# A whitening kernel: weights folded into the last matrix product, the norm given three more slots, and stores of 128 partitions, two per image, on GpSimd and at the end on SyncE

## The chip, the cores and the metric

The kernel runs on one core of one Trainium2 chip. The metric is the device time in microseconds. An execution taken with the hardware profiler gives the rows that are read below.

## What is computed

32 images of 256 channels and 48 x 48 pixels are whitened and then mixed by a 32 x 32 weight. Channel c belongs to group member c mod 32, so each image is a matrix of 32 rows and 8 x 2304 columns.

```python
x1 = x.reshape(N, C // G, G, H, W).transpose(0, 2, 1, 3, 4).reshape(N, G, -1)   # G = 32
xc = x1 - x1.mean(-1, keepdims=True)
cov = xc @ xc.transpose(0, 2, 1) / M + EPS * jnp.eye(G)
# isqrt_newton_schulz(cov, 10):
Y, Z = cov / normA, I                    # normA: the Frobenius norm
for _ in range(10):
    T = 0.5 * (3.0 * I - Z @ Y)
    Y, Z = Y @ T, T @ Z
decorr = Z / jnp.sqrt(normA)
y = weight1 @ decorr @ xc + bias1
```

## The kernel before

All is float32. An image stands in SBUF as 128 partitions of 2 x 2304 numbers (channels 0 to 127 and 128 to 255), in one of ten slots (`xs`, the trace's `image`), and the output overwrites it there. Every engine has its instructions written out by hand in one order, with semaphores between them; there is no scheduler. Images go in pairs (16 pairs). The loop of every engine runs over the pairs c, and in each over six rounds j of four slots s (24 slots). Three pairs are in work at a time:

- pair c is centred, transposed and its covariance is summed: ScalarE takes a shift off each quarter of an image (`centre`, L220), VectorE transposes it in twelve pieces (`transpose`, L315), and TensorE multiplies each transposed tile with itself (`covariance`, L432, six pieces an image, two pieces a round);
- pair c - 1 goes through the chain of small matrices, one step a slot: `chain` on TensorE (L454 to L478) and on VectorE (L324 to L389). `STEP_AT` gives each step's slot: the norm at slot 1, the first product (`NEXT_0`, L460) at slot 3, then one step a slot up to `SPREAD` at slot 23. The norm takes a product on TensorE (L457), a root on ScalarE (`root`, L236, behind two centrings of round 0), and six operations on VectorE (L349 to L357), of which the fifth, L354, writes `t_mat`, for which L460 waits. The ten Newton steps alternate products `z y` (L462) and `factor (y z)` (L464); the last one makes z alone (L466); `FOLD` multiplies z with the weight (L468); `SPREAD` puts the result on all four blocks of 32 partitions with four products and makes the offset with two (L474, L476). VectorE then writes `apply_w` (L377) and `y_bias` (L379);
- pair c - 2 is put out: `output` on TensorE (L493, four products of 384 columns for each of twelve strips) and on ScalarE (L230, which adds the bias and writes the strip into the image's slot).

Of the four output products, the one from partition half `row` to half `half` reads and writes the image half `row ^ half`. So for the first 128 channels a slot holds the output in order, and for the last 128 with its two halves of 64 partitions exchanged. GpSimd stores an image when its six strips are there (`store`, L181 to L188) by three DMAs: one of 128 partitions and two of 64. The last image is stored in three pieces of two strips. SyncE issues the loads, four quarters an image (L171). From image 10 on it waits at L170 for the stores of the image that had the slot. VectorE's `covariance_out` and `GATHER` (L339 to L345) stand at the end of a pair and are touched only by one more operation.

## Time and profile before

| what | us |
|---|---|
| median of 3 runs | 467.77 (463.84 to 476.04) |
| the profiled execution, its own time | 462.93 |
| its span, first to last instruction | 461.0 |
| TensorE busy in it | 379.3 (82%) |
| ScalarE busy | 332.9 (72%) |
| VectorE busy | 329.4 (71%) |

The engines are PE (TensorE's products), PEld (its weight loads), DVE (VectorE), ACT (ScalarE), POOL (GpSimd) and SP (SyncE); L12 is line 12 of the kernel printed above. An arrow `a<-b` in a row is an instruction that writes a and reads b. A float32 product stands in the rows as two matmuls. Busy time overlaps between engines. Idle time of an engine counts only where somebody waits for it, so the lists of waits and the timeline are read beside it. The granted clock (PEclk) is 1.00 at 2.4 GHz and 0.50 at 1.2 GHz.

### The profile page before, as it was taken

The numbers are of one execution on the slowest core, as the hardware profiler recorded it, in microseconds if no ns is written. First come the engines' busy times: TensorE is split into PE (matmuls) and PEld (weight loads), VectorE is DVE, ScalarE is ACT, GpSimd is POOL, SyncE is SP. The second block draws the span as 40 slices with busy tenths as digits, with TensorE's granted clock in tenths as the row PEclk, the third lists the DMA queues.
The fourth block names the chain that finished last, engine by engine and source line by source line (L and its number), as shares of the span: only waits on it lengthen the run. The fifth ranks groups of instructions, "written<-read, shape, count | busy, mean of one in ns | idle before, by whom it ended". The sixth has DMA issues, their size and how long they took to land.

```text
span 461.0 us, 17013 instructions
## 1 busy us (share of the span) xinstructions
PE 379.3 (82%) x7392; PEld 271.3 (59%) x7392; DVE 329.4 (71%) x1033; ACT 332.9 (72%) x450; POOL 56.8 (12%) x108
## 2 busy tenths in 40 slices
PE   0868899898989899898989897989999897977700
PEld 0856766666657667675756665666767575633100
DVE  5767887797869777988868787779888786643000
ACT  5772478797969868787878787787878796455800
POOL 0000001111111111020111111111102011112500
PEclk9976999999999989999989999899999999999965
DMA  7999939999999999999999999999999666677990
GB/s 271 416 409 410 412 141 284 338 346 351 381 358 404 357 394 344 398 390 390 385 383 362 381 394 382 367 327 388 384 391 388 218 208 208 200 213 225 312 268 18
DMA packets 28747, 152.11 MB, mean 330 GB/s; under 512 B 3968, under 2 KB 3968, under 8 KB 20736
## 3 DMA queue, kind: packets, MB, share of 16 engines
q0 software_dynamic: 9952, 75.50, 46.6%
q1 hardware_dynamic: 18432, 75.51, 43.2%
q8 instruction: 58, 0.95, 0.8%
q14 instruction: 17, 0.14, 0.1%
q10 hardware_dynamic: 288, 0.01, 0.0%
HBM read 75.51 MB, written 75.50 MB: 328 GB/s over the span
## 4 chain that ended last, share of the span: by engine, by line
PE 67%; DVE 11%; ACT 8%; issue 5%; DMA 2%; POOL 1%; SPq 0%; DVEq 0%; POOLq 0%; ACTq 0%
PE cov_ps L432 29%; PE y_ps L493 25%; PE chain_ps L464 6%; ACT image L220 6%; DVE transposed L315 5%; PE chain_ps L462 2%; DMA image<-x 2%; PE cov_ps L444 1%; PE chain_ps L474 1%; POOL y L188 1%; DVE yz L353 1%; DVE t_mat L354 1%; DVE col L350 1%; ACT image L230 1%; PE chain_ps L466 1%
## 5 line engine op out<-in xcount | busy, mean ns | idle before, releaser
L315 DVE STREAM_TRANSPOSE transposed<-image 128x384 f32<-128x384 f32 x384 | 215.7, 572 | 13.5 <-ACT image L220 2.8
L230 ACT ACTIVATE image<-y_ps,y_bias 128x768 f32<-128x768 f32 x192 | 164.8, 894 | 68.4 <-PE y_ps L493 67.7
L432 PE MATMUL cov_ps<-transposed 128*64 128x65 f32 x4608 | 178.7, 231 | 5.4 <-issue 5.4
L493 PE MATMUL y_ps<-image,apply_w 64*64 64x384 f32 x1536 | 171.8, 513 | 4.4 <-issue 2.3
L432 PEld LDWEIGHTS cov_ps<-transposed 128*64 128x64 f32 x4608 | 160.9, 142 | 14.5 <-issue 6.3
L220 ACT ACTIVATE image<-image,shift 128x1152 f32<-128x1152 f32 x128 | 156.1, 1248 | 1.8 <-DMA image<-x 0.8
L493 PEld LDWEIGHTS y_ps<-image,apply_w 64*64 64x64 f32 x1536 | 58.9, 135 | 15.1 <-ACT image L230 7.6
L186 POOL DMA_DIRECT2D y<-image x34 | 19.4, 572 | 381.1 <-ACT image L230 381.1
L462 PEld LDWEIGHTS chain_ps<-yz 128*64 128x64 f32 (+1 forms) x288 | 32.8, 138 | 35.4 <-DVE yz L367 27.3
L367 DVE SCALAR_TENSOR_TENSOR yz<-yz,chain_ps 64x96 f32<-64x96 f32 x144 | 33.8, 234 | 22.9 <-PE chain_ps L464 16.9
L464 PE MATMUL chain_ps<-yz,t_mat 64*64 64x96 f32 x256 | 47.0, 265 | 3.4 <-DVE t_mat L362 3.4
L464 PEld LDWEIGHTS chain_ps<-yz,t_mat 64*64 64x64 f32 x256 | 27.3, 135 | 35.8 <-DVE t_mat L362 28.8
L462 PE MATMUL chain_ps<-yz 128*64 128x32 f32 (+1 forms) x288 | 37.9, 213 | 6.9 <-DVE yz L359 3.4
L188 POOL DMA_DIRECT2D y<-image x68 | 36.7, 545 | 0.2 <-issue 0.2
L362 DVE SCALAR_TENSOR_TENSOR t_mat<-chain_ps,parity 64x64 f32<-64x64 f32 x144 | 27.3, 190 | 10.0 <-PE chain_ps L462 8.0
L212 ACT COPY shift<-shift_ps 128x1 f32<-128x1 f32 x32 | 5.1, 158 | 27.1 <-PE shift_ps L420 27.1
L349 DVE RECIPROCAL col<-col 64x1 f32<-64x1 f32 x16 | 2.5, 155 | 28.1 <-ACT col L236 28.1
L460 PE MATMUL chain_ps<-yz,t_mat 64*64 64x32 f32 x32 | 4.9, 234 | 20.9 <-DVE t_mat L354 20.7
L460 PEld LDWEIGHTS chain_ps<-yz,t_mat 64*64 64x64 f32 x32 | 3.1, 135 | 31.2 <-DVE t_mat L354 31.2
L420 PE MATMUL shift_ps<-shift_sum,shift_mat 128*64 128x1 f32 x128 | 9.3, 196 | 12.3 <-ACT junk L206 12.3
L420 PEld LDWEIGHTS shift_ps<-shift_sum,shift_mat 128*64 128x64 f32 x128 | 7.4, 141 | 12.4 <-ACT junk L206 6.5
L206 ACT ACTIVATE junk<-image 128x288 bf16<-128x288 f32 x32 | 13.8, 433 | 0.0
(59 smaller groups left out, 167.1 us busy)
## 6 DMA issues: line engine op xcount, KB each, us to landing
image<-x SPq DMA_DIRECT2D x128, 576.0 KB, 11.2
y<-image POOLq DMA_DIRECT2D x31, 1152.0 KB, 8.6
y<-image POOLq DMA_DIRECT2D x62, 576.0 KB, 11.0
y<-image POOLq DMA_DIRECT2D x3, 384.0 KB, 12.2
y<-image POOLq DMA_DIRECT2D x6, 192.0 KB, 11.6
b_col<-bias ACTq DMA_DIRECT2D x4, 0.1 KB, 6.3
w_nat<-weight ACTq DMA_DIRECT2D x2, 4.0 KB, 4.3
```

Of the source, the lines that this page charges most:

```text
L186: pool.dma_start(out_v[n, :, 0, cols], slot[:, 0, cols]).then_inc(stored[n % SLOTS][0], 16)
L188: pool.dma_start(out_v[n, channels, 1, cols], slot[rows, 1, cols]).then_inc(stored[n % SLOTS][1], 16)
L220: nc.scalar.activation(part, part, ACT.Identity, bias=shift[:, n % 2:n % 2 + 1]).then_inc(centred, 1)
L230: nc.scalar.activation(xs[n % SLOTS][:, :, STRIP * q:STRIP * (q + 1)], y_ps[:, f % 2, :, 0:STRIP], ACT.Identity, bias=y_bias[:, c % 2, i:i ...
L315: nc.vector.transpose(xt[q][:, TILES // 2 * part:TILES // 2 * (part + 1), 0:CH], xs[n % SLOTS][:, h, at:at + TWELFTH]).then_inc(transposed, 1)
L362: link(nc.vector.scalar_tensor_tensor(out=factor, in0=product.unsqueeze(1).to_broadcast([Q, PAIR, G]), scalar=-0.5, in1=own, op0=ALU.mult, ...
L367: link(nc.vector.scalar_tensor_tensor(out=yz[0:Q, first:YZ], in0=yz[0:Q, first:YZ], scalar=1.5, in1=following[:, first:YZ], op0=ALU.mult, ...
L420: ins = nc.tensor.matmul(shift_ps[HALF * half:HALF * (half + 1), 0:1], shift_mat[:].rearrange("p m g -> p (m g)"), shift_sum[:, n % 2:n % ...
L432: ins = nc.tensor.matmul(cov_ps[rows, n % 2, 0:GRAM], xt[q][:, t, 0:CH], xt[q][:, t, 0:GRAM], start=q == 0 and t < 2, stop=q == IMAGE_PIEC ...
L462: ins = nc.tensor.matmul(chain_ps[0:Q, C_PRODUCT:C_PRODUCT + G], z, y, start=True, stop=True)
L464: ins = nc.tensor.matmul(chain_ps[0:Q, C_NEXT:C_NEXT + YZ], factor, both, start=True, stop=True)
L493: ins = nc.tensor.matmul(y_ps[out_rows, f % 2, h, 0:STRIP], apply_w[rows, c % 2, i].rearrange("p k g -> p (k g)"), xs[n % SLOTS][rows, h, ...
```

## The change

- The steps are fewer by two. The weight (`w_t`) now stands beside y and z in one tile (`wyz`), and the last step (`LAST`) multiplies z with `w_t` and y in one product of 64 columns. VectorE makes from it `t_wide` (the last Newton factor) and `folded` (the weighted z, scaled), and `SPREAD` is one product of the two for each half of the partitions.
- The offset is no longer part of `SPREAD`. `gather` makes the means of both images (one more product), VectorE copies them into `means` (one more operation of `GATHER`), and a new step `offset` multiplies them with `apply_w` (four products of one column on TensorE, one operation on VectorE) in slot 0 of the next pair. ScalarE's first output and TensorE's next norm product wait for it (`offset_dve`).
- The norm's product goes from slot 1 to slot 2, VectorE's part to slot 4, `NEXT_0` to slot 5: three slots stand between the norm's product and `NEXT_0`. ScalarE's `root` stands behind the first evacuation of its round, no longer ahead of it, and `half_root` one round later.
- The output product from partition half `row` to half `half` now reads image half `half` and writes half `row`. So a slot holds channels r * 64 to r * 64 + 63 (first 64 partitions) and 128 + r * 64 on (last 64). One image is two DMAs (r = 0, 1), each of all 128 partitions in SBUF, and of 2 runs of 64 channels in HBM. GpSimd issues those of images 0 to 29, SyncE those of 30 (whole) and 31 (in three pieces), behind its loads.

```diff
-STEP_AT = {1: NORM, 3: NEXT_0} | {t + 1: t for t in range(NEXT_0 + 1, SPREAD + 1)}
+OFFSET_AT, NORM_AT, NORM_OUT_AT, NEXT_0_AT = 0, 2, 4, 5
...
-    out_v = out.rearrange("n (h p) a b -> n p h (a b)", h=HALVES)
+    out_v = out.rearrange("n (o r p) a b -> n r o p (a b)", o=HALVES, r=2)
...
+        def store(engine, n, pieces, signals):
+
+            engine.wait_ge(y_read, IMAGE_PIECES * n + pieces.stop)
+            cols = slice(STRIP * pieces.start, STRIP * pieces.stop)
+            for r in range(2):
+                engine.dma_start(out_v[n, r, :, :, cols], xs[n % SLOTS][:, r, cols]).then_inc(signals[r], 16)
...
+            for n in range(IMAGES):
+                load(n)
+            for n in range(IMAGES - PAIR, IMAGES):
+                for q in range(0, IMAGE_PIECES, IMAGE_PIECES // PARTS[n]):
+                    store(sp, n, slice(q, q + IMAGE_PIECES // PARTS[n]), [stored_last] * 2)
+            sp.wait_ge(stored_last, 16 * 2 * sum(PARTS.values()))
...
-                pool.dma_start(out_v[n, :, 0, cols], slot[:, 0, cols]).then_inc(stored[n % SLOTS][0], 16)
-                for rows, channels in ((slice(0, HALF), slice(HALF, P)), (slice(HALF, P), slice(0, HALF))):
-                    pool.dma_start(out_v[n, channels, 1, cols], slot[rows, 1, cols]).then_inc(stored[n % SLOTS][1], 16)
...
+            for n in range(IMAGES - PAIR):
+                store(pool, n, slice(0, IMAGE_PIECES), stored[n % SLOTS])
...
+                    if exists(c - 2):
+                        output(c - 2, 2 * j)
                     if j == 0 and exists(c - 1):
                         root(c - 1)
-                    if exists(c - 2):
-                        output(c - 2, 2 * j)
...
+                elif t == LAST:
+
+                    weighted, product = product, chain_ps[0:Q, C_PRODUCT + G:C_PRODUCT + 2 * G]
+                    link(nc.vector.scalar_tensor_tensor(
+                        out=t_wide[:], in0=product.unsqueeze(1).to_broadcast([Q, 2, G]), scalar=-0.5, in1=eye15_wide[:],
+                        op0=ALU.mult, op1=ALU.add))
+                    link(nc.vector.scalar_tensor_tensor(
+                        out=folded[:], in0=weighted.unsqueeze(1).to_broadcast([Q, PAIR, G]), scalar=RSQ, in1=own,
+                        op0=ALU.mult, op1=ALU.mult))
...
+            def offset(c):
+
+                pe.wait_ge(chain_dve, OPS_TOTAL * (c + 1))
+                for half in range(2):
+                    for i in range(PAIR):
+                        ins = nc.tensor.matmul(chain_ps[HALF * half:HALF * (half + 1), C_OFFSET + i:C_OFFSET + i + 1],
+                                               apply_w[:, c % 2, i].rearrange("p k g -> p (k g)"),
+                                               means[:, c % 2, i:i + 1], start=True, stop=True)
+                ins.then_inc(offset_pe, 1)
...
-                        h = row ^ half
-                        ins = nc.tensor.matmul(y_ps[out_rows, f % 2, h, 0:STRIP], apply_w[rows, c % 2, i].rearrange("p k g -> p (k g)"),
-                                               xs[n % SLOTS][rows, h, STRIP * q:STRIP * (q + 1)], start=True, stop=True)
+                        ins = nc.tensor.matmul(y_ps[out_rows, f % 2, row, 0:STRIP],
+                                               apply_w[rows, c % 2, i].rearrange("p k g -> p (k g)"),
+                                               xs[n % SLOTS][rows, half, STRIP * q:STRIP * (q + 1)],
+                                               start=True, stop=True)
```

The order of TensorE's instructions at the begin of a pair with all three stages, before:

```order
L432 MATMUL cov_ps<-transposed 64x65 x12
L420 MATMUL shift_ps<-shift_sum,shift_mat 64x1 x2
L432 MATMUL cov_ps<-transposed 64x65 x12
L457 MATMUL chain_ps<-col,parity 64x1
L493 MATMUL y_ps<-image,apply_w 64x384 x8
L460 MATMUL chain_ps<-yz,t_mat 64x32
L432 MATMUL cov_ps<-transposed 64x65 x12
L462 MATMUL chain_ps<-yz 64x32
L432 MATMUL cov_ps<-transposed 64x65 x12
L464 MATMUL chain_ps<-yz,t_mat 64x96
```

The same place now (L456 is the covariance, L524 the output, L485 the norm's product, L488 `NEXT_0`, L508 the offset):

```order
L456 MATMUL cov_ps<-transposed 64x65 x12
L508 MATMUL chain_ps<-means,apply_w 64x1 x4
L444 MATMUL shift_ps<-shift_sum,shift_mat 64x1 x2
L456 MATMUL cov_ps<-transposed 64x65 x12
L524 MATMUL y_ps<-image,apply_w 64x384 x4
L485 MATMUL chain_ps<-col,parity 64x1
L524 MATMUL y_ps<-image,apply_w 64x384 x4
L456 MATMUL cov_ps<-transposed 64x65 x24
L488 MATMUL chain_ps<-wyz,t_mat 64x32
L524 MATMUL y_ps<-image,apply_w 64x384 x4
L490 MATMUL chain_ps<-wyz 64x32
L524 MATMUL y_ps<-image,apply_w 64x384 x4
```

Two covariance pieces now stand between the output products and `NEXT_0`.

GpSimd's queue before, from its first store on; the three DMAs of an image (L186 once, L188 twice) recur to the end:

```order
L178 AFFINE_SELECT eye<-eye 128x128
L186 DMA y<-image 128x2304
L188 DMA y<-image 64x2304 x2
L186 DMA y<-image 128x2304
L188 DMA y<-image 64x2304 x2
```

GpSimd's queue now:

```order
L202 MEMSET eye 128x128
L204 ISA
L204 AFFINE_SELECT eye<-eye 128x128
L179 DMA y<-image 2x64x2304 x60
L88 UNCONDITIONAL_BRANCH
```

And SyncE's queue now, where before there were the loads alone:

```order
L181 UNCONDITIONAL_BRANCH
L190 DMA image<-x 128x1152 x128
L179 DMA y<-image 2x64x2304 x2
L179 DMA y<-image 2x64x768 x6
L88 UNCONDITIONAL_BRANCH
```

The sizes are those of the side that is written, slowest dimension first: a store's began with 128 or 64 and now begins with 2.

## Rows read from the trace of the kernel before

**Rows 1.** The page, busy time and share of the span by engine.

```profile
PE 379.3 (82%) x7392; PEld 271.3 (59%) x7392; DVE 329.4 (71%) x1033; ACT 332.9 (72%) x450; POOL 56.8 (12%) x108
```

**Rows 2.** Windows: length, busy PE, PEld, DVE, ACT, POOL, PEclk, DMA share, GB/s.

```profile
282.06:307.94 25.88, 23.98 (x469) 17.23 (x466) 20.54 (x64) 20.61 (x28) 3.39 (x7) 0.93 0.99 366
307.94:332.23 24.29, 22.40 (x470) 16.28 (x468) 20.43 (x64) 20.50 (x29) 3.30 (x7) 1.00 1.00 372
332.23:356.50 24.27, 22.54 (x468) 16.27 (x466) 20.43 (x64) 20.54 (x28) 3.27 (x7) 1.00 1.01 388
```

**Rows 3.** Who waited for whom: us in total, times, longest.

```profile
DVE col L349 <- ACT col L236: 28.1, 16, 3.0
PE chain_ps L460 <- DVE t_mat L354: 20.7, 14, 2.5
ACT image L220 <- DMA image<-x: 0.8, 2, 0.4
```

**Rows 4.** Timeline of two pairs: start, us, engine, line, [idle before].

```profile
287.28 1.38 PE L432 MATMUL cov_ps<-transposed 128*64 128x65 f32 x23
...
307.94 2.40 ACT L220 ACTIVATE image<-image,shift 128x1152 f32<-128x1152 f32 x2
308.53 1.48 PE L493 MATMUL y_ps<-image,apply_w 64*64 64x384 f32 x13
310.25 0.15 ACT L236 ACTIVATE col<-chain_ps 64x1 f32<-64x1 f32 x1
...
311.39 0.22 DVE L354 SCALAR_TENSOR_TENSOR t_mat<-yz,parity 64x64 f32<-64x64 f32 x1
311.66 0.30 PE L460 MATMUL chain_ps<-yz,t_mat 64*64 64x32 f32 x2 [1.66 <-DVE t_mat L354]
311.89 0.92 PE L432 MATMUL cov_ps<-transposed 128*64 128x65 f32 x24
313.05 0.24 PE L462 MATMUL chain_ps<-yz 128*64 128x32 f32 x1 [0.24 <-DVE yz L359]
```

**Rows 5.** The window with loads only, columns as in rows 2.

```profile
10.00:50.00 40.00, 29.16 (x595) 26.17 (x596) 29.36 (x82) 25.06 (x35) 0.00 (x0) 0.83 1.02 412
```

**Rows 6.** SyncE's wait for stores; timeline of image 8's store and its slot's next use.

```profile
SPq L171 <- DMA y<-image: 231.4, 44, 26.1
...
170.76 0.57 POOL L186 DMA_DIRECT2D y<-image  x1 [13.82 <-ACT image L230]
...
217.80 0.43 ACT L206 ACTIVATE junk<-image 128x288 bf16<-128x288 f32 x1
```

**Rows 7.** DMA: packets, queues (packets, MB, share of 16 engines), issues (median us to landing).

```profile
DMA packets 28747, 152.11 MB, mean 330 GB/s; under 512 B 3968, under 2 KB 3968, under 8 KB 20736
q0 software_dynamic: 9952, 75.50, 46.6%
q1 hardware_dynamic: 18432, 75.51, 43.2%
image<-x SPq DMA_DIRECT2D x128, 576.0 KB, 11.2
y<-image POOLq DMA_DIRECT2D x62, 576.0 KB, 11.0
```

**Rows 8.** Timeline of the end: image 30's first issue, the last evacuation and the last issue.

```profile
424.95 0.57 POOL L186 DMA_DIRECT2D y<-image  x1 [7.75 <-ACT image L230]
...
435.26 1.69 ACT L230 ACTIVATE image<-y_ps,y_bias 128x768 f32<-128x768 f32 x2 [0.20 <-PE y_ps L493]
...
437.81 1.07 POOL L188 DMA_DIRECT2D y<-image  x2
```

**Rows 9.** The last window in which packets move, columns as in rows 2.

```profile
451.00:452.00 1.00, 0.00 (x0) 0.00 (x0) 0.00 (x0) 0.00 (x0) 0.00 (x0) 0.50 0.06 25
```

**Rows 10.** Groups by line, with busy us and mean ns of one.

```profile
L230 ACT ACTIVATE image<-y_ps,y_bias 128x768 f32<-128x768 f32 x192 | 164.8, 894 | 68.4 <-PE y_ps L493 67.7
L466 PE MATMUL chain_ps<-yz,t_mat 64*64 64x64 f32 x32 | 5.2, 242 | 0.4 <-DVE t_mat L362 0.4
```

More of the change, by code:

```diff
@@ L113, in whiten @@
         d_col = sb("d_col", [Q, 1])
-        d_mask = sb("d_mask", [Q, PAIR])
+        means = sb("means", [P, 2, PAIR])
         outer = sb("outer", [Q, G])
@@ L150, in whiten @@
         chain_act = sem("chain_act")
+        offset_pe = sem("offset_pe")
+        offset_dve = sem("offset_dve")
         y_done = sem("y_done")
@@ L161, in quarter_of, with load @@
             return xs[n % SLOTS][:, h, QUARTER * o:QUARTER * (o + 1)]
+        def store(engine, n, pieces, signals):
[3 more added lines that the diff above has]
+                engine.dma_start(out_v[n, r, :, :, cols], xs[n % SLOTS][:, r, cols]).then_inc(signals[r], 16)
         @block.sync
         def _(sp):
-            for n in range(IMAGES):
+            def load(n):
                 for p in range(QUARTERS):
@@ L291, in _ @@
             dve.wait_ge(shift_mat_ready, 1)
-            for zeros in (yz, t_mat, parity):
+            for zeros in (wyz, t_mat, parity, means):
                 then(nc.vector.memset(zeros[:], 0.0))
@@ L302, in _ @@
             then(nc.vector.tensor_scalar(eye15[:], eye[0:Q, 0:Q], 1.5, None, ALU.mult))
-            for i in range(PAIR):
-                then(nc.vector.tensor_copy(pick[:, i], eye[0:Q, G * i:G * (i + 1)].unsqueeze(1).to_broadcast([Q, 2, G])))
+            then(nc.vector.tensor_scalar(eye15_wide[:], eye_col[0:Q, :].unsqueeze(1).to_broadcast([Q, 2, G]), 1.5, None,
+                                         ALU.mult))
+            then(nc.vector.tensor_scalar(mean_mat[:], eye_col[:].unsqueeze(1).to_broadcast([P, 2, G]), 1.0 / SAMPLES,
+                                         None, ALU.mult))
             def transpose(n, k):
@@ L398, in _ @@
                     j = s // SLOTS_A_ROUND
-                    if s in STEP_AT and exists(c - 1):
-                        chain(c - 1, STEP_AT[s])
+                    if s == OFFSET_AT and exists(c - 2):
+                        offset(c - 2)
+                    if s in DVE_AT and exists(c - 1):
+                        chain(c - 1, DVE_AT[s])
                     if s == 9 and exists(c):
@@ L469, in chain @@
                 else:
                     for half in range(2):
-                        out_rows = slice(HALF * half, HALF * (half + 1))
-                        for i in range(PAIR):
-                            at = C_SPREAD + G * i
-                            nc.tensor.matmul(chain_ps[out_rows, at:at + G], pick[:, i].rearrange("p b g -> p (b g)"),
-                                             folded[:, 0, :], start=True, stop=True)
-                        ins = nc.tensor.matmul(chain_ps[out_rows, C_OFFSET:C_OFFSET + PAIR],
-                                               folded[:].rearrange("p b g -> p (b g)"), d_mask[:],
-                                               start=True, stop=True)
@@ L479, in chain, with offset @@
-                ins.then_inc(chain_pe, 1)
+                        ins = nc.tensor.matmul(chain_ps[HALF * half:HALF * (half + 1), C_SPREAD:C_SPREAD + PAIR * G],
+                                               t_wide[:].rearrange("p k g -> p (k g)"),
+                                               folded[:].rearrange("p i g -> p (i g)"), start=True, stop=True)
+                ins.then_inc(chain_pe, 1)
+            def offset(c):
+                pe.wait_ge(chain_dve, OPS_TOTAL * (c + 1))
[5 more added lines that the diff above has]
+                ins.then_inc(offset_pe, 1)
@@ L506, in _ @@
                         covariance(PAIR * c + 2 * j // IMAGE_PIECES, 2 * j % IMAGE_PIECES)
-                    if s in STEP_AT and exists(c - 1):
-                        chain(c - 1, STEP_AT[s], slice(0, P) if exists(c) else slice(0, Q))
+                    if s == OFFSET_AT and exists(c - 2):
+                        offset(c - 2)
+                    if s in PE_AT and exists(c - 1):
+                        chain(c - 1, PE_AT[s], slice(0, P) if exists(c) else slice(0, Q))
                     ahead = PAIR * c + 1 + j // 3
@@ L514, in _ @@
                     for m in range(1, SLOTS_A_ROUND):
-                        if s + m in STEP_AT and exists(c - 1):
-                            chain(c - 1, STEP_AT[s + m], slice(0, Q))
+                        if s + m in PE_AT and exists(c - 1):
+                            chain(c - 1, PE_AT[s + m], slice(0, Q))
                         if m < 3 and exists(c - 2):
```

96 lines of the change are left out of this document (45 added, 51 removed).

## The prediction

> **What bounds the kernel now.** I read the page first: the span is 461.0 us, TensorE is busy for 82% of it, and VectorE and ScalarE for some 72% each [rows 1]. No engine is full on average, so the stages have to be told apart. The windows of single pairs show how: an undisturbed pair takes 24.29 us, of which TensorE is busy for 22.40, VectorE for 20.43 and ScalarE for 20.50 [rows 2]. TensorE is the nearest to full, and the list of waits says what it lacks: it waits for `t_mat` of L354 before L460 (20.7 us on 14 occasions), while VectorE waits before L349 for ScalarE's root (28.1 us on 16) [rows 3]. The timeline of one pair shows it as a chain: ScalarE centres two quarters from 307.94, the root at L236 stands behind them and starts at 310.25, VectorE's norm follows and starts `t_mat` at 311.39, and TensorE, whose output products began at 308.53 and took 1.48 us, starts L460 only at 311.66, 1.66 us idle; then 0.24 us more before L462 [rows 4].
>
> Some pairs take 25.88 us at a granted clock of 0.93 in place of 1.00 [rows 2]: a part of them ran at the lower level, 1.2 GHz. The trace has three such pairs in the twelve between 81 and 382 us, and each costs 25.88 - 24.29 = 1.6 us. In the one that begins at 282.06, 23 covariance products take 1.38 us from 287.28 on, where 24 take 0.92 in the pair above [rows 4].
>
> DMA is the other thing to read. Beside the pairs it moves 366 to 388 GB/s with a busy share of 0.99 to 1.01 [rows 2], hardly below the 412 GB/s of the stretch in which there are loads only [rows 5]. Yet ScalarE waits for a load only 0.8 us in all [rows 3], because the ten slots give a lead. Image 8's store is issued at 170.76; its slot, filled with image 18, is first read at 217.80, 47.0 us later [rows 6]. In these 47.0 us lie the issue (1.7 us), the landing of the store (median 11.0 us for a half) and of the load (11.2 us) [rows 7]: 24 us, so 23 us are spare. At the end ScalarE's last evacuation runs from 435.26 to 436.95, GpSimd issues until 438.9 [rows 8], the last packets move in the window 451 to 452 [rows 9], and the span goes on for 9 us more.
>
> **The change part by part.**
>
> *Norm with three free slots.* L460's product is moved behind two more covariance pieces (0.92 us each on the timeline, some 1.7 together, as their edges overlap) [rows 4]. The root goes behind one evacuation (0.894 us [rows 10]). Root: 310.25 + 0.86 = 311.1. From its start to `t_mat` ready took 311.61 - 310.25 = 1.36 us, so `t_mat` is ready at 312.5. TensorE would be there at 310.0 + 1.7 = 311.7. The wait shrinks from 1.66 + 0.24 to about 0.75 us, a gain of 1.15. What is late next is still this root, now because of ScalarE's queue. Bounds: 0 gained (if the root slips by as much as TensorE's place) and 1.9.
>
> *Weights folded into the last product.* Per pair one L462 and the L466 (242 ns [rows 10]) go, and L468 becomes a product of 64 columns; six products of the spreading become two, but four offset products and one for the means are added. I take 0.2 us for the L466, whose end overlaps with what follows, and set the other pieces equal (bounds 0 and 0.6). VectorE loses four small operations of the chain and gets three. It isn't the bound: 20.43 busy [rows 2] and the pauses between its 64 instructions (24.29 - 20.43 less about 2.2 of waits = 1.7) make 22.1.
>
> So a pair would take 24.29 - 1.15 - 0.2 = 22.9 us. Over 14 pairs that is 20 us; half of the slow-clock cost goes with the shorter idle (2.4); the first and the last pair, bound by the chain of matrices, lose a step each (1.5). Sum 24 us, if transfers keep up. An added wait is `offset_dve` ahead of L457's successor: behind it stands TensorE's whole queue, but VectorE's bias is one short operation ahead of four transposes, and a covariance piece of 0.92 us and an output stand between the offset products and that wait, so I price it at nothing (bounds 0 and 0.4 us a pair).
>
> *The stores.* Three DMAs an image become two on GpSimd. Its issue (1.7 us an image) is off the path until the end; there, with SyncE issuing, 1.1 to 2 us go, or 3 with a quicker landing. The decisive point is another. The HBM side of every new store starts with a dimension of 2 (`2x64x2304`), where every DMA of the kernel before starts with 128, 64 or 32 rows. The packets show how those are cut: SyncE's queue has 18432 packets for 128 loads, which is 128 x (128 rows + 16), and the 3968 packets under 512 B are 16 for each of the 128 loads and the 102 stores, and 6 x (32 + 16) for ScalarE's six small loads [rows 7]. So each DMA is handed out in 16 equal shares of whole rows. A division by the outermost dimension finds only 2 equal shares in the new stores. No row of before shows such a DMA, so both ways stay open: 16 shares (nothing changes) and 2. I take 2 as the likelier.
>
> The Trainium skill, "DMA: Bandwidth & Descriptors", section "Why a DMA increments its semaphore by 16 and not by 1", says that the number of engines is the largest up to 16 that divides the slowest non-1 dimension of both sides, and "Rules for kernel authors" warns of an outermost dimension under 16; by that rule these stores get 2 engines, and SyncE's always the lowest-numbered ones. The same table advises one 128-partition transfer over two on halves, which by itself would speak for the change. The trace agrees with the rule as far as it goes (16 closing packets for outer sizes 128, 64 and 32) and has no case of 2.
>
> What 2 shares cost. One engine moves 412/16 = 25.8 GB/s in the loads-only stretch [rows 5]; all of the stores' packet time gives 75.50 MB / (0.466 x 461.0 us x 16) = 22.0 GB/s [rows 7]. I take 24.
>
> At the end: images 30 and 31 are 2 x 2359 KB = 4719 KB; over 2 engines at 24 GB/s that is 98 us (91 at 25.8, 107 at 22.0), against 26 us now from the issue at 424.95 to 451.5 [rows 8, 9]. This takes the same two engines for all eight of SyncE's stores, since they come from one queue and have one form; on changing pairs each would take only its own 590/24 = 25 us, the lower bound of this term.
>
> In the middle: one share is 590 KB. Alone on its engine it takes 590/25.8 = 23 us; if the loads first take all they ask (2359/16 = 147 KB an image each 11.45 us, or 12.9 GB/s) it takes 590/12.9 = 46 us. I take 34, the middle. Loads on a shared engine land later too: 14 us for 11.2. Then issue, store and load need 1.2 + 34 + 14 = 49 us where, at 22.9 us a pair, 47.0 x 22.9/24.3 = 44.3 are there. Loads become late, and the half pair stretches to 49/47.0 x 12.15 = 12.7 us, 25.3 a pair, near the 25.1 that the twelve pairs between 81 and 382 us take on average now (with their slow stretches): the gain in the middle is given back. Bounds: all 20 us kept (store in 23 us), or 28 us a pair, 35 us lost.
>
> Sum: image 30's store starts at 424.95 - 5 (what the first and last pairs keep, with a little of the middle) = 420; 98 us of stores, 5 us for GpSimd's shares still on those two engines, 9.5 us after the last packet: span 532.5, and 1.9 around it (462.93 - 461.0): 534.4, said as **535 us**. The profiled execution (462.93) is 4.8 us under the median of the three runs, 467.77; I add nothing for that. About 2% is what a measurement of this kernel can tell from no change.
>
> **The rivals.**
>
> *A. All stores use 16 shares; faster.* 24 us from the pairs and 3 at the end: 462.9 - 27 = 436. For it: whole-row cutting by partitions would be as natural, and SBUF's side does have 128 rows. It needs 9437 KB in 22.9 us, 412 GB/s, above the 388 of any pair; the 23 us of spare lead pay for a shortfall of 1.1 us a pair over 11 pairs (12 us), else up to 12 us come back: 436 to 448.
>
> *B. Only SyncE's stores get 2 shares.* The page calls GpSimd's queue a software and SyncE's a hardware one [rows 7], so they may cut differently. Image 30's store then starts at 424.95 - 24 = 401: 401 + 98 + 9.5 + 1.9 = 510.
>
> *C. 16 shares, and the norm's wait only moves.* The root behind the evacuation slips as far as L460 does; 5 to 8 us remain of the 24: 455 to 460, within 2%.
>
> **How the numbers follow.** Forecast (2 shares on both queues) 0.58, B 0.08, A 0.28, C 0.06. Slower 0.66, faster 0.28, same 0.06. The forecast's own range is 500 to 575: from 395 + 91 + 11.4 to 450 + 107 + 15 with the bounds of the middle. As A holds more than 2 in 10, and changing pairs of engines would end near 450, the range that is to hold 8 in 10 reaches down into it: 430 to 570.
>
> **What would show it.** Right: the page's issue table has SyncE's `y<-image` landing after 50 to 95 us and GpSimd's after 25 to 45, not 11; after the last evacuation some 80 us in which no engine works and DMA's share is near 2/16 = 0.13; a wait of ScalarE's centring for `image<-x` in the pairs; SyncE waits longer for stores than 231.4 us [rows 6]. The norm step: VectorE's wait for the root before its first reciprocal falls from 28.1 us to about 20, TensorE's for `t_mat` from 20.7 to about 10; in a pair without late loads 22.9 us. Wrong: landings near 10 us and a DMA share near 1 to the end mean A; GpSimd's near 10 and SyncE's long mean B; pairs of 24 us with short landings mean C.

## The result, and the profile after

The changed kernel takes 627.25 us (median of 4 runs, 622.4 to 639.11), the kernel before beside it 467.82 (463.84 to 476.04): 1.341 times as long, 95% interval 1.327 to 1.356. The direction and the cut into two shares were forecast; 535 us and the range up to 570 were not enough. The profiled execution took 622.4 us, its span 620.5. Runs of one kernel fall into a faster and a slower group, 2 to 6% apart: ratios and intervals are of the faster runs, and the profiles of experiments 3, 4, 6, 8 and 14 are of one of the slower.

The page of the changed kernel, first the busy time (it answers to [rows 1]), then the 40 slices (15.5 us each) of clock, DMA share and GB/s:

```profile
PE 401.1 (65%) x7360; PEld 277.0 (45%) x7360; DVE 323.1 (52%) x1018; ACT 334.8 (54%) x450; POOL 47.9 (8%) x66
...
PEclk9978998968979888989879879797789997555555
DMA  8999259898989989999899899898776686311110
GB/s 311 411 411 392 72 146 267 258 305 313 300 269 304 305 263 281 336 296 276 318 331 324 288 286 309 249 270 278 231 232 210 189 220 189 107 74 50 51 52 40
```

Two losses can be seen at once. The slices 7 to 30 move 231 to 336 GB/s, where [rows 2] had 366 to 388; and in the last four some 50 GB/s are left, after TensorE's last work, at a clock of 0.5. DMA view of the changed kernel, as in [rows 7]:

```profile
DMA packets 82234, 152.31 MB, mean 245 GB/s; under 512 B 57072, under 2 KB 57072, under 8 KB 74224
## 3 DMA queue, kind: packets, MB, share of 16 engines
q0 software_dynamic: 62400, 71.00, 40.4%
q1 hardware_dynamic: 19472, 80.22, 34.1%
q8 instruction: 58, 0.95, 0.6%
...
image<-x SPq DMA_DIRECT2D x128, 576.0 KB, 18.7
y<-image POOLq DMA_DIRECT2D x60, 1152.0 KB, 42.0
```

SyncE's queue has 19472 packets: 18432 for the loads as before, and 1040 for its 8 stores, 130 each: 128 rows and 2 closing packets, not 16. So the new stores are cut in two. GpSimd's stores land after 42.0 us (11.0 in [rows 7]), the loads after 18.7 (11.2).

Windows of the changed kernel (columns as in [rows 2]); the first two are a pair's length each in the middle, the others lie behind the last evacuation, which ends at 516:

```profile
281.32:313.57 32.25, 24.57 (x453) 16.81 (x450) 20.01 (x62) 20.60 (x29) 3.14 (x4) 0.90 0.93 301
313.57:340.69 27.12, 24.71 (x477) 17.32 (x479) 20.32 (x62) 20.83 (x29) 3.14 (x4) 0.93 1.00 324
525.00:550.00 25.00, 0.00 (x0) 0.00 (x0) 0.00 (x0) 0.00 (x0) 0.00 (x0) 0.50 0.35 110
550.00:575.00 25.00, 0.00 (x0) 0.00 (x0) 0.00 (x0) 0.00 (x0) 0.00 (x0) 0.50 0.13 52
```

A DMA share of 0.13 is 2 engines of 16, and 52 GB/s over them is 26 GB/s each. Waits of the changed kernel (us in total, times, longest); L364, L488, L369 and L232 are the L349, L460, L354 and L220 of [rows 3], and L218 sums the pixels for the shift:

```profile
ACT image L232 <- DMA image<-x: 68.8, 31, 6.3
DVE col L364 <- ACT col L248: 63.9, 16, 14.1
ACT junk L218 <- DMA image<-x: 37.2, 11, 11.0
PE chain_ps L488 <- DVE t_mat L369: 15.5, 10, 5.2
```

ScalarE now waits 106 us for loads, where it waited 0.8. VectorE's wait for the root grew to 63.9 us because ScalarE reaches the root late, when a load in front of it is late: with the same order of instructions and without late loads (experiment 1) it is 18.4 us. So its length says nothing of the norm step here.

How late becomes a time is read from the chain that ended last, changed kernel (start, us, what):

```profile
281.32 37.95 DMA y<-image
...
319.28 2.08 SPq L190
...
321.41 1.88 SPq L190
...
323.33 1.85 SPq L190
...
325.22 30.92 DMA image<-x
```

Image 14's store is issued at 281.32 and lands 37.95 us later; only then SyncE issues the loads into its slot, some 2 us each, and the last quarter needed lands at 356.14, 74.8 us after the store was issued. The same piece from 196.45 on is a store of 44.95, SyncE's issues and a load of 29.14, to 277.64: 81.2 us, after which the chain comes to the store at 281.32, 3.7 us later. Between the stores of image 9 and image 14 five images pass in 84.9 us, 17 each. The last turn, from the store at 359.83 on, is longer and carries seven images: the store takes 44.18 us, then SyncE needs 51.9 us to get to the last of 12 loads (29.8 of them are waits whose end the profile can't name), and that load lands at 473.49. All of the middle goes at about one pace: GpSimd's store of image 4 is at 115.94 and that of image 25 at 462.78, 16.5 us an image, 33 us a pair.

The loss can be split in two by the kernel of experiment 1, which has 64-row halves, the same compute side and a span of 445.2 us. GpSimd's last issue starts at 504.31 in the changed kernel and at 419.40 in that one, 85 us apart; from there to the end of the span the changed kernel needs 116.2 us and the other 25.8, 90 us apart.

### The profile page after: what moved, and what is told of

It is laid out like the page before. It is cut to its first block, busy times and chain, and to the rows that moved or that the text cites. A ratio compares the mean times of both kernels' runs of the same rounds, so it can differ in the third digit from the quotient of the medians.

```text
span 620.5 us, 16900 instructions
## 1 busy us (share of the span) xinstructions
PE 401.1 (65%) x7360; PEld 277.0 (45%) x7360; DVE 323.1 (52%) x1018; ACT 334.8 (54%) x450; POOL 47.9 (8%) x66
## 2 busy tenths in 40 slices
DMA packets 82234, 152.31 MB, mean 245 GB/s; under 512 B 57072, under 2 KB 57072, under 8 KB 74224
## 3 DMA queue, kind: packets, MB, share of 16 engines
q0 software_dynamic: 62400, 71.00, 40.4%
q1 hardware_dynamic: 19472, 80.22, 34.1%
## 4 chain that ended last, share of the span: by engine, by line
DMA 46%; PE 16%; SPq 7%; another core or an unknown queue 5%; ACT 4%; DVE 3%; issue 2%; ACTq 0%; DVEq 0%
DMA y<-image 28%; DMA image<-x 18%; SPq L190 7%; PE cov_ps L456 7%; PE y_ps L524 6%; ACT image L242 2%; PE chain_ps L492 2%; ACT image L232 1%; DVE transposed L329 1%; ACT junk L218 0%; PE chain_ps L490 0%; DVE wyz L381 0%; DVE t_mat L377 0%; PE cov_ps L468 0%
## 5 line engine op out<-in xcount | busy, mean ns | idle before, releaser
L232 ACT ACTIVATE image<-image,shift 128x1152 f32<-128x1152 f32 x128 | 157.0, 1250 | 69.8 <-DMA image<-x 68.8
L524 PE MATMUL y_ps<-image,apply_w 64*64 64x384 f32 x1536 | 187.1, 553 | 10.4 <-ACT image L242 9.1
L456 PE MATMUL cov_ps<-transposed 128*64 128x65 f32 x4608 | 183.2, 236 | 10.6 <-issue 10.5
L456 PEld LDWEIGHTS cov_ps<-transposed 128*64 128x64 f32 x4608 | 166.6, 147 | 30.4 <-issue 20.0
L179 POOL DMA_DIRECT2D y<-image x60 | 47.2, 790 | 457.2 <-ACT image L242 457.1
L524 PEld LDWEIGHTS y_ps<-image,apply_w 64*64 64x64 f32 x1536 | 57.2, 142 | 20.6 <-ACT image L242 16.6
L381 DVE SCALAR_TENSOR_TENSOR wyz<-wyz,chain_ps 64x96 f32<-64x96 f32 x128 | 30.3, 237 | 53.3 <-PE chain_ps L492 53.2
L492 PE MATMUL chain_ps<-wyz,t_mat 64*64 64x96 f32 x256 | 47.5, 267 | 4.3 <-DVE t_mat L377 3.4
L492 PEld LDWEIGHTS chain_ps<-wyz,t_mat 64*64 64x64 f32 x256 | 28.5, 139 | 38.0 <-DVE t_mat L377 26.9
L490 PEld LDWEIGHTS chain_ps<-wyz 64*64 64x64 f32 (+1 forms) x256 | 30.0, 142 | 32.9 <-DVE wyz L381 18.9
L377 DVE SCALAR_TENSOR_TENSOR t_mat<-chain_ps,parity 64x64 f32<-64x64 f32 x128 | 25.4, 199 | 21.3 <-PE chain_ps L490 18.6
L490 PE MATMUL chain_ps<-wyz 64*64 64x32 f32 (+1 forms) x256 | 34.2, 216 | 3.2 <-DVE wyz L381 2.7
L364 DVE RECIPROCAL col<-col 64x1 f32<-64x1 f32 x16 | 2.5, 155 | 63.9 <-ACT col L248 63.9
L218 ACT ACTIVATE junk<-image 128x288 bf16<-128x288 f32 x32 | 14.0, 436 | 37.3 <-DMA image<-x 37.2
L224 ACT COPY shift<-shift_ps 128x1 f32<-128x1 f32 x32 | 4.9, 154 | 26.8 <-PE shift_ps L444 26.8
L488 PE MATMUL chain_ps<-wyz,t_mat 64*64 64x32 f32 x32 | 5.3, 247 | 15.6 <-DVE t_mat L369 15.5
L488 PEld LDWEIGHTS chain_ps<-wyz,t_mat 64*64 64x64 f32 x32 | 3.4, 148 | 18.2 <-DVE t_mat L369 17.9
L485 PEld LDWEIGHTS chain_ps<-col,parity 64*64 64x64 f32 x32 | 5.1, 165 | 8.7 <-issue 7.4
## 6 DMA issues: line engine op xcount, KB each, us to landing
image<-x SPq DMA_DIRECT2D x128, 576.0 KB, 18.7
```

The source lines that it names most:

```text
L179: engine.dma_start(out_v[n, r, :, :, cols], xs[n % SLOTS][:, r, cols]).then_inc(signals[r], 16)
L232: nc.scalar.activation(part, part, ACT.Identity, bias=shift[:, n % 2:n % 2 + 1]).then_inc(centred, 1)
L377: link(nc.vector.scalar_tensor_tensor(out=factor, in0=product.unsqueeze(1).to_broadcast([Q, PAIR, G]), scalar=-0.5, in1=own, op0=ALU.mult, ...
L381: link(nc.vector.scalar_tensor_tensor(out=yz[0:Q], in0=yz[0:Q], scalar=1.5, in1=following, op0=ALU.mult, op1=ALU.add))
L456: ins = nc.tensor.matmul(cov_ps[rows, n % 2, 0:GRAM], xt[q][:, t, 0:CH], xt[q][:, t, 0:GRAM], start=q == 0 and t < 2, stop=q == IMAGE_PIEC ...
L490: ins = nc.tensor.matmul(chain_ps[0:Q, C_PRODUCT:C_PRODUCT + G], z, y, start=True, stop=True)
```

## The experiments

All are edits of the changed kernel unless said otherwise, and each ran beside the kernel before on its chip (medians 463.81 us beside experiments 1 to 4, 467.95 beside 5 to 8, 470.52 beside 9 to 12, 465.53 beside 13 and 14).

**1. Every new store in two of 64 rows.**

```diff
-                engine.dma_start(out_v[n, r, :, :, cols], xs[n % SLOTS][:, r, cols]).then_inc(signals[r], 16)
+                for o in range(HALVES):
+                    engine.dma_start(out_v[n, r, o, :, cols], xs[n % SLOTS][HALF * o:HALF * (o + 1), r, cols]).then_inc(
+                        signals[r], 16)
```

with the counts of the waits for `stored` doubled.

> The changed kernel, but each of its stores is cut into two DMAs of 64 channels, so that the HBM side starts with 64 and no longer with 2; queues, layout and all of the compute stay. Theory 'shares' (the stores with an outermost dimension of 2 ran on two engines, and that alone made the kernel slower): stores land in about 11 us on GpSimd, no idle stretch at the end, 436 to 448 us, 5% under the kernel before. Rival 'compute' (the new chain, norm and offset order lose time in the middle, where pairs take 33 us in the changed kernel): pairs stay near 33 us, over 500 us.

Measured: 447.2 us (446.22 to 454.01, 4 runs), 0.963 times the kernel before, interval 0.954 to 0.972. Same bytes, same order, same issuing engines: 180 us less than the changed kernel. DMA issues of this kernel:

```profile
image<-x SPq DMA_DIRECT2D x128, 576.0 KB, 14.0
y<-image POOLq DMA_DIRECT2D x120, 576.0 KB, 9.7
y<-image SPq DMA_DIRECT2D x4, 576.0 KB, 6.4
```

The whole loss is the form of the stores. The halves also made each DMA smaller; experiment 4 leaves the size alone.

**2 and 3. Halves for GpSimd's stores only, and for SyncE's only.** GpSimd stores the images up to 29, SyncE the rest, so the edit of experiment 1 goes under a condition, and the other engine keeps 2 x 64:

```diff
+                if n < IMAGES - PAIR:
```

and in the second kernel `n >= IMAGES - PAIR`.

> As rows64, but only GpSimd's stores (images 0 to 29) are cut into 64 channels; SyncE's for the last pair keep the outermost dimension of 2. 'Shares': the middle is that of rows64, the last evacuation comes near 410, and then two engines need 4719 KB / 52 GB/s = 91 us from image 30's issue on: 500 to 510 us. Rival 'SyncE's long end only follows from GpSimd's backlog on the same engines': then the end shrinks to some 20 us and the time is 440 to 455.

Measured: 530.65 us (529.51 to 531.79), 83 us over experiment 1. GpSimd's stores land after 9.2 us, the last evacuation ends at 437.9, and the page's last slices move 46 to 59 GB/s: the tail alone. The 500 to 510 us that I expected were too few, because the last evacuation was to end near 410.

> As the changed kernel, but SyncE's stores of the last pair are cut into 64 channels; GpSimd's keep the 2. 'Shares': the middle stays as in the changed kernel (last evacuation near 515), then 15 to 25 us until the last packet: 535 to 550 us. So the two parts of the loss are about 80 us each, and rows64_gpsimd and rows64_synce together account for it.

Measured: 554.46 and 584.67 us; I compare 554.46, 107 us over experiment 1. In the profiled run, that of 584.67, GpSimd's stores land after 44.0 us and ScalarE's centring waits 115.4 us for loads. The parts, 83 and 107, make 190 us where the whole loss is 180: both queues cut by the outermost dimension, and within the spread of these runs the two losses add.

**4 to 6. Other outermost dimensions with whole-tile stores.** One number differs, `o=HALVES` in `out_v` becomes 16, 4 or 8 (the output's rows then come in another order). The three texts stand in the order 16, 4, 8.

> The changed kernel with one number changed: the HBM side of a store is (16, 8, columns) and no longer (2, 64, columns), still 128 partitions and two DMAs an image. Rows land on other channels than they should, all of them once, so the output is permuted. 'Shares by the outermost dimension': 16 shares, landing near 11 us, within 1% of rows64. Rival 'a store whose HBM side is not one even run of rows is slow' (the pattern, not the first number): it stays near 620 us.

Measured: 448.95 us (440.52 to 456.09), ratio 0.954 (0.939 to 0.969). The 128-partition store is as good as two halves once its HBM side starts with 16.

> The HBM side of the stores is rearranged as 4 x 32 rows instead of 2 x 64; the rows of the output come out in another order, every byte count and every wait is as in the changed kernel. Theory (engines = shares of the outermost dimension, and the loss is made of late slots): 4 engines a store, so SyncE's tail is 4719 KB over 4 x 26 GB/s = 45 us instead of 91-100, from image 30's store at 405 to 425 on (the kernel with 64-row halves issues it at 425.8). In the middle a share is 295 KB; GpSimd's stores land in 18 to 25 us, loads in 12 to 14, so issue + store + load = 32 to 41 us, under the 47 that are spare: pairs stay near 24 us. Together 460 to 485 us, and the packets of SyncE's 8 stores are 8 x (128 + 4). Rival 1 (the small packets that a GpSimd store of few shares puts on the other engines cost time of their own, and there are 12/14 x 33/65 of them, 0.44 as many): 0.44 of the 78 us lost in the middle stay, 34 us more: 495 to 520. Rival 2 (only the number 2 is special): near the 447 of the halves kernel.

> As before with 8 x 16 rows on the HBM side (output rows in another order). Theory: 8 engines, a share of 147 KB, tail 4719 KB over 8 x 26 GB/s = 23 us, which is about what the two last images take with all 16 engines beside the last loads and evacuations; GpSimd's stores land in 11 to 14 us. 445 to 458 us. Rival 1 (small packets): 0.15 of 78 us stay, 12 us more: 457 to 470. SyncE's packets are 8 x (128 + 8).

Measured: 546.5 us with 4 shares (2 runs, ratio 1.170, 1.159 to 1.182), and 495.77 and 526.9 us with 8, of which the run of 526.9 was profiled. Both lie far over the forecast of the theory, and the loss is not where the rival put it: ScalarE's centring waits for loads only 0.9 and 0.5 us. What waits is TensorE, and for nothing that the profile shows. Chain by engine, kernel with 8 shares:

```profile
PE 65%; issue 14%; DVE 8%; ACT 5%; DMA 2%; SPq 0%; ACTq 0%; DVEq 0%
```

Here 14% is 74 us; the kernel before has 4.7% of 461, 22 us. With 4 shares the longest piece is this, in the middle of a group of output products (timeline of TensorE, then the DMA view of 340 to 342 us, the same kernel):

```profile
333.58 0.83 PE L524 MATMUL y_ps<-image,apply_w 64*64 64x384 f32 x3
344.08 0.90 PE L524 MATMUL y_ps<-image,apply_w 64*64 64x384 f32 x2 [9.67 <-issue]
```

```profile
q8 instruction: 1, 0.02, 3.0%
```

Nothing stands between two products of one group except the next instruction. The page has a queue q8 of kind "instruction" with 58 packets in every kernel that has a program on TensorE, and its 0.95 MB make 16 KB a packet; in the four kernels without one (experiments 9, 10, 13 and 14) this queue is not there. Looked up microsecond by microsecond, its packets mostly come 4 to 9 us apart; where a long stall is, one is late, and the stall ends 2 to 3 us behind it. With 4 shares the packets after 318 us are in the microseconds from 318, 325 and 341, and the stall ends at 344.08; the five other stalls of 5 to 8.7 us end at 127.6, 162.8, 184.8, 233.4 and 446.8, with packets from 125, 160, 182, 231 and 444 on. With 8 shares the longest, 7.21 us, ends at 308.7, and the packet is in 306 to 307. It holds without exception: each of TensorE's issue waits of more than 1 us, 15 with 4 shares and 18 with 8, ends 2.4 to 3.4 us after the begin of a packet's microsecond. So TensorE stops for its code. That the code is late because the stores' shares load the DMA engines is what experiment 12 tests. In profiled spans the kernel with 4 shares has its last evacuation end 62 us later than experiment 1 (493.5 for 431.4) and needs 38 us more from there to its end; with 8 shares these are 66 and 14. TensorE's issue waits are 46 us more in both profiles (64 for 18): they are most of what was lost ahead of the last evacuation in these runs.

**7. Nine slots in the changed kernel** (`SLOTS = 9`).

> The changed kernel with 9 image slots in place of 10. From a slot's first read to its store's issue the kernel before needs 5 pairs less 47.0 us, i.e. 74.5 us or 3.07 pairs of 24.29 us; what is left of the slot's cycle is issue + store + load, L. With 10 slots the cycle is 5 pairs, so a pair takes L / 1.93; the changed kernel has L = 1.7 + 42.0 + 18.7 = 62.4 us, which gives 32.3 us a pair (33 are measured in the middle). Theory 1 (the time is set by lateness, landing times fixed by the shares): with 9 slots the cycle is 4.5 pairs, a pair takes 62.4 / 1.43 = 43.6 us, 10.6 us more over some 12 pairs: about 750 us, with landings still near 42 and 18.7. Theory 2 (the two engines a store and the small packets set a throughput, and the landing times are only what queues up): pairs stay at 33 us, 615 to 640 us, and landings fall by 16.5 us together, to some 30 and 14. Between the two: a pair of 36 to 39 us, 670 to 700, if landings fall by part.

Measured: 687.81 and 706.47 us, median 697.1; stores land after 41.5 us and loads after 18.2, as with ten slots; 18.6 us an image (37.2 a pair). Chain of this kernel:

```profile
229.63 46.73 DMA y<-image
276.75 2.12 SPq L190
278.91 2.64 SPq L190
281.59 22.67 DMA image<-x
307.94 39.60 DMA y<-image
347.56 14.03 DMA image<-x
363.34 43.05 DMA y<-image
```

A throughput that alone sets the pace is out: the landings did not shorten, and the time rose by 70 us. From store to store the chain takes 78.3 us from 229.63 to 307.94, about what it took with ten slots (84.9), but only four images pass in it, not five. My scaling of the wait by pairs (43.6 us a pair) was too steep, which comes back below; the later turns of 55 to 58 us carry three images.

**8. The root ahead of the evacuation again**, on top of experiment 1.

```diff
-                    if exists(c - 2):
-                        output(c - 2, 2 * j)
                     if j == 0 and exists(c - 1):
                         root(c - 1)
+                    if exists(c - 2):
+                        output(c - 2, 2 * j)
```

> The kernel with 64-row halves of every new store (447.2 us) in which ScalarE's root stands ahead of the evacuation again, as in the kernel before, while TensorE's norm product keeps its three free slots. Theory of the prediction (the root behind the evacuation is what ends VectorE's wait): the root comes 0.9 us earlier, t_mat is ready before TensorE asks for it, and the rest of the wait goes: 0.4 to 0.7 us a pair over 14 pairs, 437 to 442 us. Rival (in the changed kernel TensorE loses its time elsewhere, to y_ps waits and issue gaps, and the evacuation that is now held behind the root starts late): 445 to 455, no difference that can be measured.

Measured: 453.68 us (4 runs: 441.02, 453.0, 454.36 and 456.93). This decides nothing: the median is with the rival, the shortest run with the theory, and it is 5 us under the shortest of experiment 1. In the profile, of the run of 456.93, VectorE's wait for the root falls from 18.4 to 7.0 us, but TensorE's issue waits are 29.9 us (17.9 in experiment 1), and these 12 us more are above the 6 to 10 that the step was to give.

**9 and 10. The transfers alone**: the programs of ScalarE, VectorE and TensorE are left out, a store waits for its image's loads.

> ScalarE's, VectorE's and TensorE's whole programs are left out: SyncE loads, GpSimd and SyncE store what was loaded, with the changed kernel's ten slots, queues, sizes and 2 x 64 forms. What is left is the transfers alone. Theory 1 (in the changed kernel the loss in the middle is lateness; the transfers themselves would carry more): a slot's cycle is now issue + store + load = 62.4 us for ten images, 6.2 us an image, so the middle is bound by bytes (388 GB/s: 12.2 us an image for 4.72 MB both ways) and the whole takes about 390 us plus a tail of SyncE's stores on two engines (4719 KB at 52 GB/s = 91 us less the 12 that two images take anyway): 460 to 490 us. Theory 2 (two engines a store and the small packets set a throughput of 16.5 us an image whatever the compute engines do): 30 x 16.5 + 91 + 12 = 590 to 620 us.

> The same without compute, with every new store cut in two of 64 rows (16 engines each). Bound by bytes: 151 MB at 380 to 400 GB/s is 378 to 397 us, with the start and the end 390 to 415 us. It gives the price of the 2 x 64 form in transfers alone: theory 1 above says 70 to 80 us more for the other kernel, theory 2 some 200.

Measured: 542.1 and 383.7 us. Between the two theories: windows 100:300 of the two kernels, the 2 x 64 one first (us, POOL busy, clock, DMA share, GB/s):

```profile
100.00:300.00 200.00, 23.80 (x31) 1.00 1.04 338
```

```profile
100.00:300.00 200.00, 35.95 (x68) 1.00 1.02 407
```

GpSimd's first store is issued at 9.70 and image 29's at 394.50, 26.5 us a pair, against 23.6 with halves (10.57 to 352.35). So the transfers alone would allow 26.5 us a pair. The 33 of the changed kernel are lateness above that, and part of the loss is a lower throughput: the engines are as busy and move 17% less.

**11 and 12. The computation alone**: 11 is the kernel before, 12 the changed kernel with the halves of experiment 1 for its last pair. In both the stores of images 0 to 29 are left out, and a load waits for the last evacuation in its slot.

> The kernel before without the stores of images 0 to 29 (a load into a slot waits for the last evacuation of the image in it): the computation alone, with half of the transfers. The pair of 24.29 us should stay, since no wait in it is for a transfer: 440 to 465 us. TensorE's short issue stalls (0.79 us in a pair) stay if they are its own, and go if they come from its code being loaded behind the data.

> The changed kernel's computation with 64-row halves for the last pair's stores and no stores of images 0 to 29. The prediction's terms for norm and weights alone: pairs of 22.9 us, 20 to 24 us less than the same cut of the kernel before. Theory 3 (TensorE stops for its own code, which is loaded by the same DMA engines in pieces of 16 KB, and stops longer the longer the shares of the stores stand in front of it): without the stores TensorE's issue waits, 17.9 us on 19 occasions with longest 3.6 in the halves kernel, fall below 8 us with none above 1.5. Rival (they belong to the new order of TensorE's instructions): they stay at 15 to 20 us.

Measured: 447.98 and 426.88 us, 21.1 apart. Windows of one pair, kernel before and then changed kernel:

```profile
208.45:232.73 24.28, 22.39 (x469) 16.27 (x466) 20.42 (x64) 20.50 (x28) 0.00 (x0) 1.00 0.50 175
```

```profile
245.65:268.85 23.20, 22.23 (x461) 15.64 (x461) 19.77 (x63) 20.53 (x29) 0.00 (x0) 1.00 0.52 189
```

and the product `NEXT_0` in the second, L487 there (TensorE's timeline, with the wait ahead of it):

```profile
245.65 0.24 PE L487 MATMUL chain_ps<-wyz,t_mat 64*64 64x32 f32 x1 [0.89 <-DVE t_mat L368]
```

TensorE's issue waits fall to 1.8 us on 2 occasions, from 17.9 on 19 in experiment 1, and in the kernel before from 7.9 us on 12 to 2.8 on 2, while q8 still brings 58 packets: they come from what the stores do to the loading of its code, not from its own order. The chain still has one issue piece of 0.90 us in every pair, as the kernel before has one of 0.79 with its stores and without.

**13 and 14. The transfers alone with 4 and with 8 shares.**

> The transfers alone (no program on ScalarE, VectorE and TensorE) with the stores as 4 x 32 rows. The whole kernel of this form took 546 us, 99 more than with halves, while its engines hardly waited for data and TensorE's issue waits were 64 us. Theory A (most of the loss is TensorE waiting for its own code behind the stores' shares): the transfers alone are only little slower than with halves (384 us): a middle at 370 to 400 GB/s and a tail of 45 us in place of 12: 410 to 435 us. Theory B (the transfers of this form are slow in themselves): 470 us or more.

> The same with 8 x 16 rows. The whole kernel of this form took 496 to 527 us, 50 to 80 more than with halves. Theory A: 385 to 400 us (tail 23 us in place of 12). Theory B: 430 us or more.

Measured: 460.6 us (454.3 to 466.95) and 395.4 (390.74 to 400.08). With 8 shares that is as theory A has it; with 4 it is between the two, nearer to B. Beside 383.7 with 16 shares, the transfers alone lose 12 us with 8 shares, 77 with 4 and 158 with 2; the whole kernels lose 49 to 80, 99 and 180 against 447.2. With 8 shares most of the loss is therefore not in the transfers themselves, whose middle moves 406 GB/s, as with 16 shares (407). In the profiled run, 80 us over experiment 1, 46 us of it are TensorE's issue waits; for the run 49 us over it there is no profile. With 4 both hold: the tail is longer, the middle (100 to 300 us) moves 377 GB/s in place of 407, and the issue waits are the same. How these share the 99 us I can't say, as they overlap.

## Why the prediction missed the size

**Compute side: right, with two sizes off that offset.** A pair of 22.9 us was forecast, 23.20 was measured, and 21.1 us over the whole where the sum had 24. So a pair gives 1.08 us, not 1.35 (which over 14 pairs makes 18.9 us; the sum had it as 20). The clock gave more than its term: between ScalarE's roots at 58.08 and 378.58 experiment 11 has 13 pairs, of which three take 25.88 us at a granted clock of 0.93; the 13 of experiment 12, to 360.41, are all at 1.00. All of the 4.8 us of the slow stretches went, where the sum had half of them, 2.4, without a row for it. The wait before `NEXT_0` was to be 0.75 us and is 0.89, still the root behind an evacuation; without stores VectorE's wait for the root goes from 26.8 to 16.7 us (28.1 to about 20 was forecast) and TensorE's for `t_mat` from 24.1 to 13.2. That rival C would hold is excluded by 21.1 us.

**Two shares: right, on both queues.** Experiments 1 and 4 exclude other causes of the whole loss, 2 and 3 find a part of it in each queue. Rival A's condition did not hold; its time (436 to 448) is what the same kernel needs once the stores have 16 shares, 447.2 and 448.95. Rival B fell with experiment 3. The Trainium skill, "DMA: Bandwidth & Descriptors", section "Why a DMA increments its semaphore by 16 and not by 1", has k as the largest divisor of both slowest dimensions up to 16; the trace agrees, with 2, 4, 8 and 16 closing packets a SyncE store for 2, 4, 8 and 16 rows (130, 132, 136 and 144 packets a store).

**The tail: right in sum, in part by luck.** Forecast 98 + 5 + 9.5 = 112.5 us from image 30's first issue to the end of the span; measured 620.5 - 510.57 = 109.9. One of the two engines moves 28 GB/s until about 620, 6 us after the other, and nothing follows it: the 9.5 us behind the last packet are not there. At the 52 GB/s of the rows above the 4719 KB take 91 us, not 98. By this estimate some 18 us are left for what GpSimd's stores still had on these two engines, where the sum had 5. Where the 9 us of the kernel before come from is open: in experiment 11, where GpSimd issues the last stores too, the last packets move in the window 443 to 444 and the span ends at 445.6.

**The middle: the step that failed.** Image 30's store was to be issued at 420 and is issued at 510.57; these 90.6 us are the whole error (622.4 - 534.4 = 88). The step is the sum issue + store + load of 1.2 + 34 + 14 = 49 us, measured 81.2 and 74.8 on the chain in the two turns from 196.45 and from 281.32. Each piece was too small, the load most of all:
- the store lands after 45 and 38 us there (47 and 44 in two other places of the chain), near the upper bound of 46 that I gave, not at 34. I took the middle of two bounds, though loads fill the engines;
- the load lands after 29 and 31 us there, not 14. I raised the median from 11.2 to 14 (the median became 18.7); the chain doesn't meet medians, it follows the latest quarter. That this is the one whose engines carry a store's share is likely, but no row shows it;
- SyncE's issues were missing. Its load issue, 0.33 us at best, has a median of 1.33 and reaches 6.85 us; a slot's loads cost 6 to 7 us in these two turns, and 9 in the one from 76.20.

The rule that turned the sum into a time, 49/47.0 of a pair, was right in kind (a delay divides itself over the images of a turn, experiment 7) and wrong in size. It took the 47.0 us to the first read of the slot's next image. The chain goes through the last quarter, which in the kernel before is read 55.1 us after the store's issue at 170.76, and the turn closes with the store five images on, image 13's:

```profile
225.87 1.25 ACT L220 ACTIVATE image<-image,shift 128x1152 f32<-128x1152 f32 x1
...
230.19 0.57 POOL L186 DMA_DIRECT2D y<-image  x1 [9.13 <-ACT image L230]
```

With the measured 75 to 81 us and the 3.7 us from a late load to the next store, five images in a turn give 16 to 17 us each, 31 to 34 a pair, as measured; my proportion would give 39 to 42. So the two errors work against each other, and my upper bound shows how luck could have hidden this: with the store at 46 the sum is 1.2 + 46 + 14 = 61.2 us, and the proportion gives 31.6 us a pair (not the 28 that I wrote as bound), nearly the 33 measured. By the turn of five images the same 61.2 us make 26 a pair. The store's bound alone would not have been enough; the load had to be right too.

**What I had not in the sum at all:** a lower throughput of such stores (experiment 9), and TensorE's code behind them (below). The second shows little in the changed kernel: its chain has 2% of issue, 14 us, of which one stall of 5.1 us ends at 176.15; that its code arrives while TensorE waits for loads anyway is my explanation, which no run tests. It may also be why 16 shares give 16.6 us in the whole kernel (463.81 - 447.2) and not the 21.1 of the computation alone, as TensorE's issue waits are 17.9 us in experiment 1 and 7.9 in the kernel before; but the interval of experiment 1 reaches from 13 to 21 us. The kernel before has this loss too, unread by me: three of its pairs, from root to root, take 25.57 to 25.68 us at a clock of 1.00, and experiment 11 has none such.

## What to carry to other kernels

Count the outermost dimension of both sides of a DMA before joining two into one: a rearranged view that starts with 2 puts a whole tile on two engines, and one store of 128 partitions is then worse than two of 64, here by 180 us on 447. Where buffers turn around through store, issue and load, price a delay by the latest piece of each on the chain, not by medians, count the turn to the last piece that is read and not to the first, and divide it by the images that pass in it; a bound that the loads' own traffic makes likely is not to be averaged away. If TensorE stops in the middle of a group with "issue", look for the packets of the instruction queue before looking at its order.

## What the runs showed of the hardware

- **Code loading can stop TensorE.** The stalls reach 9.67 us with 4 shares, 7.21 with 8, 5.1 with 2, 3.7 with 16, and 1.6 without stores; with 16 shares their sum is 17.9, 24.8 and 29.9 us in experiments 1, 4 and 8. The Trainium skill, "Runtime: NRT & Kernel Launch", section "Instruction fetch mechanics", says that code is streamed in 16 KiB blocks through the sequencer's own DMA queue and that this is mostly hidden. The 58 packets of 16 KB agree; that it is hidden does not hold here under loaded engines. Why 8 shares stall it as much as 4 (64 us in both, one profile each) is open.
- **A GpSimd store with 2 shares seems to touch all 16 engines.** This is worked out from counts; no row tells the engines apart. Its queue has 62400 / 60 = 1040 packets a store, 16 x 65. The 57072 packets under 512 B are 60 x (14 x 65 + 2) and 2048, 16 and 288 of the loads, SyncE's stores and ScalarE's loads: as if each of the 14 engines without rows got 65 small packets as well. A store's packets are 528, 272 and 144 with 4, 8 and 16 shares, which is 16 x 33, 16 x 17 and 16 x 9. SyncE's stores don't do this. I can't tell what they cost: no experiment removed them alone.
- **SyncE's issue is held up behind few shares.** Its 8 stores of 2 shares take 681 ns to 32.97 us each to issue, 90.76 us together (row below, changed kernel). The longest issue of such a store is 33.0 us with 2 shares, 14.8 with 4, 4.6 with 8 and 2.0 with 16. Whatever stood behind them on SyncE would come that late.

```profile
L179 SPq DMA_DIRECT2D y<-image x8: 681/7448/32970, 510.6 to 593.9; - x8
...
DMA to landing us min/median/max: 26.8/42.0/79.8
```
